# A DLRM tower: four of 32 fields looked up by one-hot products on TensorE, the others gathered field by field

## The reference

```python
e = jnp.stack([tbl_0[ids[:, 0]], ..., tbl_31[ids[:, 31]]], axis=1)      # [2048, 32, 256]
dots = jnp.einsum('bnd,bmd->bnm', e, e)
z = dots[:, iu, ju]                                                      # pairs i < j
h = jnp.concatenate([z, dense_ctx], axis=1)                              # [2048, 512]
h = jnp.maximum(h @ W_top1 + b_top1, 0.0)                                # 512 -> 512
h = jnp.maximum(h @ W_top2 + b_top2, 0.0)                                # 512 -> 256
y = h @ W_top3                                                           # 256 -> 1
```

## Time and profile before

| | |
|---|---|
| median of 3 runs | 672.66 us (671.53 to 675.78) |
| the profiled execution | 671.6 us, span 669.8 us |
| granted TensorE clock, share of 2.4 GHz | 0.781 |
| busy: PE, PEld, POOL | 502.9, 416.9, 484.8 us |
| busy: DVE, ACT | 203.6, 164.8 us |
| DMA | 71.65 MB, mean 107 GB/s |

### The profile page before, as it was taken

One profiled execution on the slowest core, in us unless ns is written; L12 is line 12 of the kernel. 1 busy time (PEld: TensorE's weight loads), 2 busy tenths in 40 slices (PEclk: granted clock), 3 DMA queues, 4 the chain that ended last, 5 costly groups with the idle time before them and its releaser, 6 DMA issues.

```text
span 669.8 us, 23188 instructions
## 1 busy us (share of the span) xinstructions
PE 502.9 (75%) x10560; PEld 416.9 (62%) x10560; DVE 203.6 (30%) x564; ACT 164.8 (25%) x321; POOL 484.8 (72%) x518
## 2 busy tenths in 40 slices
PE   2668778696886968778696877959679696877847
PEld 1547567485764847567485755848567484755736
DVE  0213433204343132433304343231433313343330
ACT  1222213222142222313222141222313222141310
POOL 6777777777777777777777777777777777777730
PEclk9857859687696877859688695977959597696958
DMA  7333333333333333333333333333333333333310
GB/s 246 109 104 111 107 107 109 106 109 106 106 110 104 111 106 107 109 104 112 105 107 110 104 112 104 108 109 103 111 106 109 108 104 109 106 108 109 105 57 0
DMA packets 26753, 71.65 MB, mean 107 GB/s; under 512 B 9232, under 2 KB 10144, under 8 KB 26528
## 3 DMA queue, kind: packets, MB, share of 16 engines
q0 software_dynamic: 24576, 67.14, 34.4%
q1 hardware_dynamic: 2080, 3.03, 1.3%
HBM read 70.13 MB, written 0.01 MB: 105 GB/s over the span
## 4 chain that ended last, share of the span: by engine, by line
POOL 38%; PE 25%; issue 15%; DMA 11%; DVE 9%; ACT 2%; SPq 0%; ACTq 0%
POOL rows L121 38%; PE ps_l L160 15%; DMA rows<-in_table,index 11%; DVE pairs L240 9%; PE ps_turn L134 6%; PE ps_gram L147 3%; ACT hidden L216 1%; PE ps_l L172 1%; ACT cols L207 1%; DMA raw<-in_index_t 0%; DVE hidden L251 0%; PE ps_l L179 0%; SPq L84 0%; DVE score L257 0%; ACTq L35 0%
## 5 line engine op out<-in xcount | busy, mean ns | idle before, releaser
L121 POOL DMA_INDIRECT rows<-in_table,index x512 | 484.1, 946 | 157.6 <-issue 142.2
L240 DVE COPY pairs<-ps_gram 32x128 f32<-32x128 f32 (+1 forms) x512 | 188.2, 368 | 422.9 <-PE ps_gram L147 416.4
L134 PE MATMUL ps_turn<-identity,rows 128*128 128x128 f32 x1024 | 207.1, 336 | 135.2 <-DMA rows<-in_table,index 134.6
L207 ACT COPY cols<-ps_turn 128x512 f32<-128x512 f32 x256 | 148.8, 590 | 482.5 <-PE ps_turn L134 482.5
L134 PEld LDWEIGHTS ps_turn<-identity,rows 128*128 128x128 f32 x1024 | 135.0, 167 | 158.1 <-DMA rows<-in_table,index 139.8
L160 PE MATMUL ps_l<-pairs,w_sb 128*128 128x128 f32 x1024 | 149.3, 319 | 22.6 <-DVE pairs L240 22.6
L160 PEld LDWEIGHTS ps_l<-pairs,w_sb 128*128 128x128 f32 x1024 | 146.2, 233 | 24.6 <-DVE pairs L240 24.5
L147 PEld LDWEIGHTS ps_gram<-cols 128*32 128x32 f32 x8192 | 104.8, 126 | 62.7 <-issue 55.3
L147 PE MATMUL ps_gram<-cols 128*32 128x32 f32 x8192 | 135.5, 214 | 4.3 <-ACT cols L207 3.6
L172 PE MATMUL ps_l<-hidden,w_sb 128*128 128x128 f32 x256 | 32.8, 281 | 1.2 <-ACT hidden L216 1.2
L172 PEld LDWEIGHTS ps_l<-hidden,w_sb 128*128 128x128 f32 x256 | 29.8, 191 | 2.0 <-ACT hidden L216 1.4
(11 more groups left out here) (3 smaller groups left out, 0.3 us busy)
## 6 DMA issues: line engine op xcount, KB each, us to landing
rows<-in_table,index POOLq DMA_INDIRECT x512, 2.7
w_sb<-in_w_t SPq DMA_DIRECT2D x1, 2048.0 KB, 8.6
w_sb<-in_W_top SPq DMA_DIRECT2D x1, 512.0 KB, 10.9
pairs<-in_dense_t SPq DMA_DIRECT2D x16, 8.0 KB
scores<-score SPq DMA_DIRECT2D x16, 0.5 KB
raw<-in_index_t SPq DMA_DIRECT2D x1, 248.0 KB, 2.6
base<-in_base_t SPq DMA_DIRECT2D x1, 0.5 KB, 2.0
raw<-in_index_t SPq DMA_DIRECT2D x1, 8.0 KB, 1.8
```

What stands on the lines that cost most here:

```text
L121: pool.indirect_dma_start(out=rows[u % ROWS][:, k, :], out_offset=None, in_=table, in_offset=bass.IndirectOffsetOnAxis(ap=index[:, q:q + 1 ...
L134: last = pe.transpose(ps_turn[u % 2][:, h, k, :], rows[u % ROWS][:, k, h * P:(h + 1) * P], identity[:, :])
L207: act.copy(cols[u % COLS][:, :, :, :], ps_turn[u % 2][:, :, :, :]).then_inc(cols_ready, 1)
L240: last = dve.tensor_copy(pairs[n % 2][N_FIELDS * q:N_FIELDS * (q + 1), c0:KC, TQ * j + FQ * u:TQ * j + FQ * (u + 1)] .rearrange("p c g -> ...
```

## The change

Four fields with 1000 rows (the last four of them in order, `PICKS`) are no longer gathered. Their tables are loaded whole into SBUF, 125 partitions by 8 rows, and each is split into two F32R parts: `table_hi` is the rounded table (a ScalarE copy), `table_lo` what is left (a TensorE product with the identity and one with its negative, four pieces per table, `split_table`, copied out by VectorE). For a job of one such field and 256 samples, TensorE spreads the 256 ids over 125 partitions (`spread_ids`), VectorE compares them with the row numbers into a one-hot matrix (`make_one_hot`, eight instructions of 256 columns), and TensorE multiplies it by both parts (`pick`, 2 halves x 8 chunks x 2 parts = 32 products of 256 columns). There are 32 jobs. ScalarE copies each to `stage` (`take_pick`) and later, per block of 64 samples, into `cols` (`place`).

The other 28 fields are gathered in another order: a gather now brings 32 samples of four fields. A unit is four fields of a block of 64 samples, still two gathers and four transposes, and a block has seven units, 224 units in all. There are 8 row buffers instead of 16. The columns of `cols` lie field by field, 64 samples each, so ScalarE's copies read and write without steps, and the 32 columns of one sample, which a Gram product takes as both operands, lie 64 elements (256 bytes) apart. A Gram product can only start when its whole block is there. The pairs' numbering follows the new order of fields through the host's arrangement of the first layer's weights.

The core of the diff (the SyncE loads, the semaphores and the host's arrangement are left out):

```diff
+    UNITS = (N_FIELDS - PICKS) // FPU
+    SUBS = BLOCK // SPG
+    GATHERS = UNITS * SUBS
+    BLOCKS = index_t.shape[1] // GATHERS
+    FQ, TQ = BLOCK // QUAD, P // QUAD
+    TILES = BLOCKS // 2
+    BPG = GROUP // BLOCK
+    JOBS = pick_ids.shape[0]
...
+    V = pick_tables[0].shape[0]
+    VC = 8
+    VP = V // VC
+    ROWS, COLS = 8, 3
+    PIECES = VC * D // 512
...
-        rows = [sb(f"rows{r}", [P, UQ, D]) for r in range(ROWS)]
-        cols = [sb(f"cols{r}", [P, HALVES, UQ, P]) for r in range(COLS)]
...
+        rows = [sb(f"rows{r}", [P, SUBS, D]) for r in range(ROWS)]
+        cols = [sb(f"cols{r}", [P, HALVES, N_FIELDS, BLOCK]) for r in range(COLS)]
+        stage = [sb(f"stage{g}", [P, HALVES, PICKS, GROUP]) for g in range(2)]
...
+                for u in range(UNITS):
+                    x = UNITS * t + u
+                    if x >= ROWS:
+                        pool.wait_ge(transposed, x - ROWS + 1)
...
-            def transposes(u):
-                pe.wait_ge(gathered[u % ROWS], 16 * UQ * (u // ROWS + 1))
-                if u >= 2:
...
+                if x >= 2:
+                    pe.wait_ge(cols_ready, x - 1)
                 for h in range(HALVES):
-                    for k in range(UQ):
-                        last = pe.transpose(ps_turn[u % 2][:, h, k, :],
-                                            rows[u % ROWS][:, k, h * P:(h + 1) * P], identity[:, :])
+                    for k in range(SUBS):
...
+                                            rows[x % ROWS][:, k, h * P:(h + 1) * P], identity[:, :])
                 last.then_inc(transposed, 1)
 
-            def gram(u):
-                f = u // UPF
-                pe.wait_ge(cols_ready, u + 1)
-                if u % UPF == 0 and f >= 2:
-                    pe.wait_ge(pairs_ready, f - 1)
-                for k in range(UQ):
+            def split_table(j):
+                pe.wait_ge(hi_ready, j + 1)
+                raw_v = table_raw[j].rearrange("p c d -> p (c d)")
+                hi_v = table_hi[:, j, :, :].rearrange("p c d -> p (c d)")
+                for i in range(PIECES):
+                    x = PIECES * j + i
+                    if x >= 2:
+                        pe.wait_ge(lo_ready, x - 1)
+                    pe.matmul(ps_low[x % 2], identity[0:VP, 0:VP], raw_v[:, 512 * i:512 * (i + 1)],
...
+                    pe.matmul(ps_low[x % 2], minus_identity[0:VP, 0:VP], hi_v[:, 512 * i:512 * (i + 1)],
+                              start=False, stop=True).then_inc(low_done, 1)
+
+            def spread_ids(q):
+                pe.matmul(ps_ids[0:VP, 0:GROUP], identity[0:JOBS, q:q + 1].broadcast_to([JOBS, VP]), pick_id_f[:, :],
+                          start=True, stop=True).then_inc(ids_spread, 1)
+
+            def pick(q, h):
+                j = q % PICKS
+                if h == 0:
+                    pe.wait_ge(one_hot_ready, q + 1)
+                    if q + 1 < JOBS:
+                        spread_ids(q + 1)
+                    if q < PICKS:
+                        pe.wait_ge(lo_ready, PIECES * (j + 1))
+                    if q >= 1:
+                        pe.wait_ge(stage_ready, q)
+                for c in range(VC):
+                    pe.matmul(ps_pick[:, h, :], table_hi[:, j, c, h * P:(h + 1) * P], one_hot[q % 2][:, c, :],
+                              start=(c == 0), stop=False)
+                    last = pe.matmul(ps_pick[:, h, :], table_lo[:, j, c, h * P:(h + 1) * P], one_hot[q % 2][:, c, :],
+                                     start=False, stop=(c == VC - 1))
+                if h == HALVES - 1:
+                    last.then_inc(picked, 1)
+
+            def gram(b, part):
+                if part == 0:
+                    pe.wait_ge(cols_ready, UNITS * (b + 1))
+                    pe.wait_ge(picks_placed, b + 1)
+                    if b >= 2:
+                        pe.wait_ge(pairs_ready, b - 1)
+                for g in range(FQ // 2 * part, FQ // 2 * (part + 1)):
                     for h in range(HALVES):
                         for j in range(QUAD):
-                            x = cols[u % COLS][:, h, k, N_FIELDS * j:N_FIELDS * (j + 1)]
-                            last = pe.matmul(ps_gram[f % 2][N_FIELDS * j:N_FIELDS * (j + 1), UQ * (u % UPF) + k, :],
+                            x = cols[b % COLS][:, h, :, QUAD * g + j]
+                            last = pe.matmul(ps_gram[b % 2][N_FIELDS * j:N_FIELDS * (j + 1), g, :],
                                              x, x, start=(h == 0), stop=(h == HALVES - 1))
-                last.then_inc(gram_done, 1)
+                if part == 1:
+                    last.then_inc(gram_done, 1)
 
             def layer1(n):
-                pe.wait_ge(pairs_ready, FPT * (n + 1))
+                pe.wait_ge(pairs_ready, 2 * (n + 1))
                 pe.wait_ge(dense_loaded[n % 2], 16 * (n // 2 + 1))
                 if n == 0:
...
-            for u in range(UNITS):
-                transposes(u)
-                if u >= 1:
-                    gram(u - 1)
-                n, at = u // UPT - 1, u % UPT
-                if n >= 0:
-                    if at == 2:
-                        layer1(n)
-                    if at == UPF + 1:
-                        layer2(n)
-                    if at == UPF + 4:
-                        layer3(n)
-            gram(UNITS - 1)
...
+            spread_ids(0)
...
+            for t in range(BLOCKS):
+                for u in range(UNITS):
+                    transposes(UNITS * t + u)
+                    if t == 0 and u >= UNITS - PICKS:
+                        split_table(u - (UNITS - PICKS))
+                    if t == 1 and u < PICKS:
+                        pick(u, 0)
+                        pick(u, 1)
+                    if t == 2 and u == 0:
+                        gram(0, 0)
+                        gram(0, 1)
+                    if t >= 2 and u in (1, 2):
+                        gram(t - 1, u - 1)
+                    if t >= 3 and t % 2 == 1:
+                        if u == 1:
+                            layer2((t - 3) // 2)
+                        if u == 3:
+                            layer3((t - 3) // 2)
+                    q = PICKS + 2 * ((t - 1) // 2)
+                    if 1 <= t and q < JOBS:
+                        if t % 2 == 1 and u >= 4:
+                            pick(q + (u - 4) // 2, (u - 4) % 2)
+                        if t % 2 == 0 and u == 3:
+                            pick(q + 1, 1)
+                    if t >= 2 and t % 2 == 0 and u == 6:
+                        layer1((t - 2) // 2)
+            gram(BLOCKS - 1, 0)
...
-            def evacuate(u):
-                act.wait_ge(transposed, u + 1)
-                if u >= COLS:
-                    act.wait_ge(gram_done, u - COLS + 1)
-                act.copy(cols[u % COLS][:, :, :, :], ps_turn[u % 2][:, :, :, :]).then_inc(cols_ready, 1)
+            def evacuate(t, u):
+                x = UNITS * t + u
+                act.wait_ge(transposed, x + 1)
+                if u == 0 and t >= COLS:
+                    act.wait_ge(gram_done, t - COLS + 1)
+                act.copy(cols[t % COLS][:, :, FPU * u:FPU * (u + 1), :], ps_turn[x % 2][:, :, :, :]
+                         ).then_inc(cols_ready, 1)
+
+            def take_pick(q):
+                act.wait_ge(picked, q + 1)
+                act.copy(stage[q // PICKS % 2][:, :, q % PICKS, :], ps_pick[:, :, :]).then_inc(stage_ready, 1)
+
+            def place(b):
+                act.wait_ge(stage_ready, PICKS * (b // BPG + 1))
+                if b >= COLS:
+                    act.wait_ge(gram_done, b - COLS + 1)
+                s = BLOCK * (b % BPG)
+                act.copy(cols[b % COLS][:, :, N_FIELDS - PICKS:N_FIELDS, :],
+                         stage[b // BPG % 2][:, :, :, s:s + BLOCK]).then_inc(picks_placed, 1)
 
             def relu1(n):
                 act.wait_ge(l1_done, n + 1)
...
+                        act.copy(table_hi[:, j, :, :], table_raw[j]).then_inc(hi_ready, 1)
+                    evacuate(t, u)
+                    if t == 1 and u < PICKS:
+                        take_pick(u)
+                    if t == 1 and u == PICKS:
+                        place(0)
+                    if t >= 2 and u == 0:
+                        place(t - 1)
+                    q = PICKS + 2 * ((t - 1) // 2)
+                    if 1 <= t and q < JOBS:
+                        if t % 2 == 1 and u == 5:
+                            take_pick(q)
+                        if t % 2 == 0 and u == 3:
+                            take_pick(q + 1)
+                    if t >= 2 and t % 2 == 0 and u == 6:
+                        relu1((t - 2) // 2)
...
+            def make_one_hot(q):
+                dve.wait_ge(ids_spread, q + 1)
+                if q >= 2:
+                    dve.wait_ge(picked, q - 1)
+                for c in range(VC):
```

(88 more changed lines are left out.)

101 lines of the change are left out of this document (65 added, 36 removed).

## The result

The changed kernel takes **1016.58 us** (median of 4 runs, 1012.25 to 1022.14) against 672.33 for the kernel before beside it: ratio 1.511, 95% interval 1.503 to 1.519. The forecast was 691 us, with a range up to 770. The direction was right and the size was not.

The account below looks back on a forecast made before the run. Gathers on GpSimd set the time before; after the change TensorE's queue would, at 37.2 us per pair against GpSimd's 35.0. Start, pairs and end gave 641 us, plus 50 for the column step: 691 us, range 618 to 770.

Parts of the forecast that it names:

- free step: Gram products reading columns 256 bytes apart at no extra cost; the whole kernel was then forecast at 641 us.
- column step: Gram products read both operands with 256 bytes between columns: +50 us taken, low end 0, +100 if loading and streaming double.
- S = 1.5: Factor on Gram product time if the streaming part doubles, taken as nearest to VectorE's regrouping copy: +50 us.
- My last line: Said the forecast is wrong if four interleaved strided streams hinder each other more than one does, which would lie above 761.
- The base: Forecast of the whole changed kernel without any cost for the column step: 641 us.
- the 4.8 us of waits: TensorE's waits for VectorE per pair of blocks in the new order: 2.9 us plus 1.9 us, within 37.2 us.
- The two waits that I named: TensorE waits 2.9 us for the next one-hot in odd blocks and 1.9 us at layer 1 in even blocks.
- all cases get longer: What follows if the granted clock falls into the 1.2 GHz level in TensorE's 2 to 3 us waits for VectorE.
- The 4.1 MB of table loads cost nothing: At the start, table loads move like the 2048 KB of weights and land in 17 us, adding no time.
- its 11 us as an estimate: With 5 engines for 125 partitions, the last table would land near 40 us and everything some 11 us later.
- Rival C: F32R pick products stream at the f32 column rate, 0.23 us for 256 columns: 760 to 810 us; chance 0.14.
- Rival A: The Gram products' column step is free: 641 us, or 612 if TensorE's waits vanish; chance 0.34.

Follow-up runs that it names:

- e2: The changed kernel, but each Gram product takes 32 neighbouring columns (wrong ones, same work) as both operands, with layout and writes unchanged: 797.16 us.
- e10: The changed kernel with fields 272 bytes apart, the second one-hot's job moved behind the hand-off and `place` to the end of its own block: 672.66 us.
- e7: The changed kernel with columns laid sample by sample (827.01 us), and each table load cut into 112 and 13 partitions: 813.08 us.

## Why the prediction was wrong

In spans, the forecast had 638.9 us with a free step; e2 has 795.4, the changed kernel 1016.0. The direction owes little to the sum: with a free step it had the kernel faster, and e2 is slower too.

**The column step was mis-sized: forecast +50 us, measured +219.** The failed step is "S = 1.5", taken from VectorE's regrouping copy. That row costs about two per element at 512 bytes. For the Gram products 1.5 would have been fair at 16 and at 272 bytes (1.4); at 256 the factor is 3.5 (391.9 / 112.5). My last line allowed for more than 761 us, if four streams hinder each other more than one does, and gave that no price and no chance; whether it is the four streams no run shows. The 219 us (220.6 in spans) come about so. TensorE is busy for 875.0 us in place of 608.2 in e2: +279 for the Gram products (391.9 in place of 112.5), and -13 for the rest of its work, at a granted clock of 0.928 in place of 0.903. It is idle for 141.0 in place of 187.2 us, -46, of which 37 are the "issue" holes in the Gram products (39.4 us in e2, 2.5 here).

**The base was mis-sized: forecast 641, measured 797.** By place it is +31 at the start (layer 1 of the first tile at 115.9 in place of 85.1), 13 x (45.4 - 37.2) = +107 in the pairs, and +19 at the end. One pair by parts, the one whose rows are shown above in part (the means of 13 pairs are 59.8, 45.4 and 36.6):

| us per pair | forecast | after | e2_step1 | e10_order |
|---|---|---|---|---|
| Gram products | 6.2 (9.3) | 25.4 | 7.3 | 9.1 |
| waits and holes | 4.8 | 7.0 | 8.5 | 0.4 |
| all other work | 26.2 | 26.2 | 29.5 | 25.9 |
| sum | 37.2 (40.3) | 58.6 | 45.3 | 35.4 |

The work was costed to within 0.3 us per pair where the clock stays at its 2.4 GHz level in these pairs. What failed is the 4.8 us of waits. The two waits that I named are there almost as computed (2.5 to 2.8 for the one-hot, forecast 2.9; 1.8 to 2.0 at layer 1, forecast 1.9). Not named were ScalarE's hand-offs: relu, evacuation and `place` stand in one list, and TensorE waits for it 1.4 and 0.8 us ahead of the Gram products and 0.4 ahead of a transpose; I had put ScalarE down as "nothing" for its idle share. A third part is holes in the dense Gram products that the profile calls issue (39.4 us in e2). And in e2 the clock is at its 1.2 GHz level for a while behind a wait: its picks after the one-hot wait are 0.21 us apart, its layer 1 lasts 8.9 in place of 7.3. I wrote of this that "all cases get longer" and put no number on it; it is 3.3 us of e2's pair (29.5 against 26.2). It doesn't follow every wait: in the changed kernel, behind the same wait of 2.5 us at 340.03, the picks are 0.12 us apart. e10 is the test: with the waits out the clock is at 0.972, and a pair falls from 45.9 to 36.6 us on average.

**The start.** "The 4.1 MB of table loads cost nothing here if they move like the 2048 KB of weights": they didn't. The first spread that waits for a one-hot stood at 64.8 us, forecast 42.5, here in the changed kernel:

```profile
64.78 0.69 PE L199 MATMUL ps_ids<-pick_id_f,identity 32*125 32x256 f32 x2 [3.48 <-DVE one_hot L373]
```

The roundings started at 18.9, 30.5, 44.6 and 54.3 us, the last three after a wait for their loads, and the first three splits began at the 1.2 GHz level (pieces 2.3 us apart where 1.1 is the price). e7 shows 14 of the 31 us. The rule of the Trainium skill that I had quoted (DMA: Bandwidth & Descriptors, on why a DMA increments its semaphore by 16) has 5 engines for 125 partitions, and 16 for 112; its 11 us as an estimate stand beside 14 measured. The shares of the load queue agree with it, 25.5% against 82.6%; the estimate of 40 us for the last table was low, for its rounding started at 54.3. I left the rule out of the sum.

**Right.** TensorE's queue became the bound and GpSimd waited for its transposes, though for 251.9 us, not 75. Rival C is refuted: picks stand 0.12 us apart at the 2.4 GHz level, as taken from the nearest row. Rival A's time of 641 needs both a free step and short waits; even e2 didn't have it. The end was much as thought, the last gather 54 us before the end (forecast 45). ScalarE's and GpSimd's stretched instructions lie beside the Gram products and end with them, so they seem to cost little themselves; no run took them apart.

**What stays open.** Which multiples of which distance are bad, and whether a single stream would pay too; why half blocks at 256 bytes differ among themselves (5.3 to 6.9 us); why the same wait brings the clock down in e2 and not in the changed kernel; and 17 of the 31 us at the start, which e7 does not give back.

## What to carry to other kernels

Before laying out a buffer that TensorE will read with a step, look at the bytes between its columns: 256 cost 3.5 times the product's time here and 272 only 1.4, for four unused elements per row. When an engine's queue becomes the bound, walk all hand-offs into it, those from mostly idle engines too, and price each wait twice, for itself and for the lower clock that can follow it. A load over 125 partitions was worth splitting here, for 14 us.

## What was unexpected of the hardware

**TensorE's reads can hold up other engines.** During a half block with 256 bytes between columns a contiguous ScalarE copy took mostly 5.4 to 7.2 us in place of 0.59, and a gather up to 6.2 in place of 0.95. Windows of the changed kernel: four half blocks, the second and the fourth with VectorE at work (busy time of PE, PEld, DVE, ACT, POOL, then clock, DMA share, GB/s).

```profile
137.90:143.30 5.40, 5.37 (x129) 5.35 (x129) 0.00 (x0) 5.19 (x1) 2.89 (x3) 1.00 0.34 100
323.50:330.20 6.70, 6.70 (x129) 6.63 (x128) 6.70 (x2) 6.57 (x1) 6.02 (x2) 1.00 0.03 6
344.50:351.37 6.87, 6.87 (x128) 6.81 (x129) 0.00 (x0) 6.87 (x1) 5.97 (x3) 1.00 0.18 50
744.05:749.38 5.33, 5.33 (x130) 5.28 (x129) 4.88 (x2) 5.22 (x1) 2.28 (x3) 1.00 0.27 79
```

In the second window the DMA engines moved almost nothing, 6 GB/s, while GpSimd got through two gathers. The other engines are held up, but it isn't VectorE's work that makes a half block long: without it one took 5.4 us and another 6.9, with it 6.7 and 5.3. With 272 bytes the copy (593 ns), the gather (946 ns) and VectorE's instructions (347 ns each) are back to their usual times.

**Dense small products run into holes.** The waits of e2 show 36 stops of TensorE in its Gram products, 39.4 us in all, the longest 2.3, with nothing waited for; slower products (after) have 6 stops and 2.5 us. The instruction queue of the profile moved 91 packets, 1.49 MB, so 16 KB each. The Trainium skill (Advanced Engine Details and Errata, ISA Cache) has lines of 16 KB or 256 instructions; that size agrees. The trace of e2 speaks for the stops being waits for such a line: 28 of the 36, 36.2 of the 39.4 us, end 1.2 to 1.6 us after one of these packets has landed, and from one to the next lie about 126.5 records of products, or a whole multiple of that, each record with a weight load of its own. The other 8 stand right behind transposes. In e10 all 18 stops, 14.5 us, end so. No run varied the instructions' number or size.
